# Linear attention in a twelve-stage network: two of TensorE's products and GpSimd's row gathers change places in the written order

## The chip, the cores and the metric

One core of one Trainium2 chip runs the whole program. The time is device microseconds (us) for one launch. TensorE is called PE, VectorE DVE, ScalarE ACT, GpSimd POOL and SyncE SP, as in the profile.

## The reference, cut to what matters

The network has twelve stages on x of 4096 tokens by 128 features: a feed-forward, an attention and a feed-forward, four times over. The change touches the fifth stage only, a causal linear attention with 16 heads of 8 features:

```python
x = x + 0.5 * _L1_ffn_ref(_layernorm(x), ...)      # stage 4: experts, two of 16 per token
x = x + _L1_attn_ref(_layernorm(x), ...)           # stage 5: the one that is changed
x = x + 0.5 * _L1_ffn_ref(_layernorm(x), ...)      # stage 6

def _L1_attn_ref(x, wq, bq, wk, bk, wv, bv, wo, bo):
    q = feature_map(x @ wq + bq); k = feature_map(x @ wk + bk); v = x @ wv + bv   # 16 heads of 8
    def step(carry, qkv):                          # over the tokens of one sequence
        S = S + k v^T; z = z + k                   # per head
        return (S, z), (q S) / (q z + 1e-6)
    return out @ wo + bo                           # feature_map(x) = x + 1 where x > 0, else exp(x)
```

## The kernel before, in words

x stays in on-chip memory for the whole program. It is cut into 8 chunks (NC) of 512 tokens, each of 4 tiles (TPC) of 128 tokens and two sequences of 256. Matrix products are in float32. Each engine has its own written-out instruction order, and semaphores are all that ties the orders to each other: an engine that waits holds up whatever stands behind it in its own order.

In the linear attention every engine loops over `g`, with `c, t = divmod(g, 4)`: chunk c, step t. While chunk c is scored and weighed, chunk c+1 is projected and chunk c+2 is fetched and normalised. The functions by engine:

- POOL, `att1_gpsimd`: before the loop it gathers the expert results of chunks 0 and 1 (`fetch_results`, L1319, 8 indirect DMAs each) and clears two buffers (L1749). In the loop, for chunk c: step 0 `widen(c)` (L1741), step 2 `key_heads(c + 1)` (L1731, the keys laid out by head) and then `ln_rstd(c + 2)` (L148 and L150, the reciprocal root for the normalisation, called the root here), step 3 `fetch_results(c + 4)`. The loop begins with c = -2, so that chunk 2 is gathered in it at c = -2 and chunk 7, the last, at c = 3. `fetch_results(i)` waits until DVE has written that chunk's row numbers (`name_result_rows`, L1328) and has used the buffer's earlier rows.
- DVE, `att1_vector`: `mask` each step (L1583), step 0 `invert(c)` (L1592, L1594), then `combine_results(c + 2)` (L1345, L1355, L1364) and `name_result_rows(c + 4)` (L1328); step 1 `divide(c - 1)` (L1601) and `map_qk(c + 1)` (L1550); step 2 `ln_stats(c + 2)` and `add_out(c - 1)` (L1605, L1609); step 3 `ln_apply(c + 2)` (L191), `add_bias` (L1558), `multiply_sums` (L1565) and `states` (L1572) of c + 1.
- PE, `att1_tensor`: `score` each step (L1473, 32 pairs of weight load and product) and at the step's end `weigh` of the step before (L1490, 32 pairs, and for the odd tiles the state's product L1496). Besides: step 0 `turn(c + 1)` (L203) and `sum_heads(c)` (L1449); step 1 `project(c + 1)` (L1391, L1394) and `spread(c)` (L1458); step 2 `values(c + 1)` (L1405 and L1408, 136 pairs), `turn_k(c + 1)` (L1416) and `project_out(c - 1)` (L1505); step 3 `token_values(c + 1)` (L1423), `sum_keys(c + 1)` (L1431, L1433) and, after `weigh`, `states(c + 1)` (L1441).
- ACT, `att1_scalar`: `copy_later` each step (L1666), `ln_copy` (L214), `exps` (L1675, L1677), `copy_spread` (L1701), `place_values` (L1688) and `token_keys` (L1695). For the first two chunks `place_values` waits for POOL's first `key_heads`.

`sum_heads(c)` waits for DVE's `states(c)`, `invert(c)` waits for `sum_heads(c)`, and `score` of a chunk's first step waits for that chunk's `key_heads`. All of `turn`, `project` and what follows for chunk 0 waits for its root.

Of the kernel before, what the change touches and what calls it, by code (L numbers as in the profile page):

```python
# [16 lines left out]
NC = N // CH  # L17
# [27 lines left out]
def tiles(ap, inner=P):  # L45
    return ap.rearrange("p (t d) -> p t d", d=inner)
# [1325 lines left out]
def att1_tensor(k, s):  # L1372
# [135 lines left out]
    for g in range(-TPC, STEPS1 + TPC):  # L1508
        c, t = divmod(g, TPC)
        if 0 <= g < STEPS1:  # L1510
            score(g)
        if t == 0 and 0 <= c + 1 < NC:
            turn(c + 1)
        if t == 0 and 0 <= c < NC:
            sum_heads(c)
        if t == 1 and 0 <= c + 1 < NC:
            project(c + 1)
        if t == 1 and 0 <= c < NC:
            spread(c)
        if t == 2 and 0 <= c + 1 < NC:  # L1520
            values(c + 1)
            turn_k(c + 1)
        if t == 2 and 0 <= c - 1 < NC:
            project_out(c - 1)
        if t == 3 and 0 <= c + 1 < NC:
            token_values(c + 1)
            sum_keys(c + 1)
        if 0 <= g - 1 < STEPS1:
            weigh(g - 1)
        if t == 3 and 0 <= c + 1 < NC:  # L1530
            states(c + 1)


def att1_vector(k, s):

    V, v, cols = k.nc.vector, k.v, k.w["L1_cols"]
    for at in (0, 3):
        v.count(V.tensor_scalar(cols[:, at + 1:at + 2], cols[:, at:at + 1], -1.0, None, ALU.mult))
        m = V.tensor_scalar(cols[:, at + 2:at + 3], cols[:, at:at + 1], 1.0, None, ALU.add)
    m.then_inc(k.sem("l1_cols"), 1)  # L1540

    def map_qk(c):
        for at, name in enumerate(("q", "k")):
            out, tmp = k.sb(f"l1_{name}{c % 2}", [P, CH]), k.sb(f"l1_exps{at}", [P, CH])
            V.wait_ge(k.sem("l1_exps"), 2 * c + at + 1)
            if at == 0 and c >= 2:
                V.wait_ge(k.sem("l1_weighed"), (c - 1) * TPC)
            if at == 1 and c >= 2:
                V.wait_ge(k.sem("l1_k_heads"), c - 1)
            V.scalar_tensor_tensor(out=out[:, :], in0=k.bank[1 + at][:, :], scalar=cols[:, 3 * at + 2:3 * at + 3], in1=tmp[:, :],  # L1550
                                   op0=ALU.add, op1=ALU.max).then_inc(k.sem("l1_mapped"), 1)

    def add_bias(c):
        v_tok = k.sb("l1_v_tok", [P, BPC * P])
        V.wait_ge(k.sem("l1_sums"), 4 * c + 1)
        if c:
            V.wait_ge(k.sem("l1_sums"), 4 * c - 1)
        V.tensor_tensor(tiles(v_tok[:, :]), tiles(k.bank[2][:, 0:BPC * P]),  # L1558
                        k.w["L1_bv"][:, :].unsqueeze(1).broadcast_to([P, BPC, P]), ALU.add).then_inc(k.sem("l1_parts"), 1)

    def multiply_sums(c):
        V.wait_ge(k.sem("l1_sums"), 4 * c + 2)
        if c:
            V.wait_ge(k.sem("l1_sums"), 4 * c)
        V.tensor_tensor(k.sb("l1_prod", [P, CH])[:, :], k.bank[1][:, :], k.sb(f"l1_q{c % 2}", [P, CH])[:, :],  # L1565
                        ALU.mult).then_inc(k.sem("l1_parts"), 1)

    def states(c):
        V.wait_ge(k.sem("l1_sums"), 4 * c + 3)
        if c >= 2:  # L1570
            V.wait_ge(k.sem("l1_weighed"), (c - 1) * TPC)
        V.tensor_tensor(tiles(k.sb(f"l1_state{c % 2}", [P, BPC * P])[:, :]), tiles(k.bank[2][:, S:S + BPC * P]),  # L1572
                        k.w["own_head"][:, :].unsqueeze(1).broadcast_to([P, BPC, P]), ALU.mult).then_inc(k.sem("l1_parts"), 1)

    def mask(g):

        V.wait_ge(k.sem("l1_scored"), g + 1)
        if g >= 2:
            V.wait_ge(k.sem("l1_weighed"), g - 1)
        for r in range(4):  # L1580
            if r >= 2:
                V.wait_ge(k.sem("l1_copied"), 4 * g + r - 1)
            V.tensor_tensor(own_blocks(k.sb(f"l1_weights{g % 2}_{r}", [P, CH])), own_blocks(k.bank[4 + r]),  # L1583
                            k.w["block_upto"][:, :].unsqueeze(1).broadcast_to([P, BPT, BLK]),
                            ALU.mult).then_inc(k.sem("l1_masked"), 1)

    def invert(c):
        inverse = k.sb("l1_inverse", [P, TPC * H])
        V.wait_ge(k.sem("l1_sums"), 4 * c + 4)
        if c:  # L1590
            V.wait_ge(k.sem("l1_wide"), c)
        v.count(V.tensor_scalar(inverse[:, :], k.bank[2][:, 0:TPC * H], 1e-6, None, ALU.add))  # L1592
        V.wait_ge(v.sem, v.n)
        V.reciprocal(inverse[:, :], inverse[:, :]).then_inc(k.sem("l1_inverse"), 1)  # L1594

    def divide(c):
        V.wait_ge(k.sem("l1_weighed"), (c + 1) * TPC)
        V.wait_ge(k.sem("l1_spread_in"), c + 1)
        if c:
            V.wait_ge(k.sem("l1_out"), c)  # L1600
        V.tensor_tensor(k.sb("l1_att", [P, CH])[:, :], k.bank[3][:, :], k.sb(f"l1_spread{c % 2}", [P, CH])[:, :],  # L1601
                        ALU.mult).then_inc(k.sem("l1_att"), 1)

    def add_out(c):
        v.count(V.tensor_tensor(tiles(k.chunk(c)), tiles(k.chunk(c)),  # L1605
                                k.w["L1_bo"][:, :].unsqueeze(1).broadcast_to([P, TPC, D]), ALU.add))
        V.wait_ge(v.sem, v.n)
        V.wait_ge(k.sem("l1_out"), c + 1)
        V.tensor_tensor(k.chunk(c), k.bank[0][:, :], k.chunk(c), ALU.add).then_inc(k.sem("x_done"), 1)  # L1609

    name_result_rows(k, s, 0)
    name_result_rows(k, s, 1)
    for g in range(-2 * TPC, STEPS1 + TPC):
        c, t = divmod(g, TPC)
        if 0 <= g < STEPS1:
            mask(g)
        if t == 1 and 0 <= c - 1 < NC:
            divide(c - 1)
        if t == 0 and 0 <= c < NC:
            invert(c)  # L1620
        if t == 0 and 0 <= c + 2 < NC:
            combine_results(k, s, c + 2)
            if c + 4 < NC:
                name_result_rows(k, s, c + 4)
        if t == 1 and 0 <= c + 1 < NC:
            map_qk(c + 1)
        if t == 2 and 0 <= c + 2 < NC:
            ln_stats(k, s, c + 2, s.results0 + c + 3)
        if t == 2 and 0 <= c - 1 < NC:
            add_out(c - 1)  # L1630
        if t == 3 and 0 <= c + 2 < NC:
            ln_apply(k, s, c + 2)
        if t == 3 and 0 <= c + 1 < NC:
            add_bias(c + 1)
            multiply_sums(c + 1)
            states(c + 1)


def own_blocks(buffer):

    return blocks_at(buffer, 0, BPT, BLK)
# [79 lines left out]
def att1_gpsimd(k, s):  # L1721

    G = k.nc.gpsimd

    def key_heads(c):

        kk, k_heads = k.sb(f"l1_k{c % 2}", [P, CH]), k.sb(f"l1_k_heads{c % 2}", [P, 4 * CH])
        G.wait_ge(k.sem("l1_mapped"), 2 * c + 2)
        if c >= 2:
            G.wait_ge(k.sem("l1_scored"), (c - 1) * TPC)  # L1730
        G.tensor_tensor(k_heads[:, :].rearrange("p (b j n) -> p b j n", j=4, n=BLK),  # L1731
                        tiles(kk[:, :], BLK).unsqueeze(2).broadcast_to([P, CH // BLK, 4, BLK]),
                        k.w["every_fourth"][:, :].unsqueeze(1).unsqueeze(3).broadcast_to([P, CH // BLK, 4, BLK]),
                        ALU.mult).then_inc(k.sem("l1_k_heads"), 1)

    def widen(c):

        G.wait_ge(k.sem("l1_inverse"), c + 1)
        if c:
            G.wait_ge(k.sem("l1_spread"), c)  # L1740
        G.tensor_copy(k.sb("l1_wide", [P, CH])[:, :].rearrange("p (n d) -> p n d", d=HD),  # L1741
                      k.sb("l1_inverse", [P, TPC * H])[:, :].unsqueeze(2).broadcast_to([P, TPC * H, HD])
                      ).then_inc(k.sem("l1_wide"), 1)

    fetch_results(k, s, 0)
    fetch_results(k, s, 1)
    G.wait_ge(k.sem("x_done"), s.x0)
    for n in range(2):
        G.memset(k.sb(f"l1_v_heads{n}", [P, 4 * CH])[:, :], 0.0)  # L1749
    for g in range(-2 * TPC, STEPS1 + TPC):  # L1750
        c, t = divmod(g, TPC)
        if t == 0 and 0 <= c < NC:
            widen(c)
        if t == 2 and 0 <= c + 1 < NC:
            key_heads(c + 1)
        if t == 2 and 0 <= c + 2 < NC:
            ln_rstd(k, s, c + 2)
        if t == 3 and 2 <= c + 4 < NC:
            fetch_results(k, s, c + 4)

# [1782 lines left out]
```

## Time and profile before

| | us |
|---|---|
| median of 3 runs | 3316.7 |
| lowest, highest | 3314.06, 3324.93 |
| the profiled execution | 3320.21 |
| its span, first to last instruction | 3318.9 |
| PE busy | 2633.5 |
| DVE busy | 2105.9 |
| ACT busy | 1785.2 |
| POOL busy | 1148.0 |

The linear attention runs from about 808 us of the span (its first DVE instruction) to about 1058 us. In a timeline row the columns are the start, the length, the engine, the line, the operation and its operands, how many instructions are merged, and in square brackets how long the engine had been idle and what ended that. "issue" there means that the engine waited for nothing that the profile shows; "remote" that the wait ended on a semaphore whose sender had long finished by the profile.

### The profile page before, as it was taken

How to read it: one execution, taken by the hardware profiler on the slowest of the kernel's cores; microseconds unless marked ns; L12 is line 12 of the kernel's file. 1: busy time of each engine (PE TensorE's matmuls, PEld its weight loads, DVE VectorE, ACT ScalarE, POOL GpSimd, SP SyncE). 2: the span in 40 equal slices, each digit the busy share in tenths (PEclk: the TensorE clock that was granted, in tenths of full speed). 3: DMA queues.
4: the chain of work that ended last, by engine and by line, in shares of the span. 5: the costliest groups of instructions: out<-in, count | busy, mean ns of one | idle time of the engine just before them, and what ended most of it. 6: DMA issues, size and time to landing. Idle time of an engine off the chain costs nothing. (4 is left out here: it accounts for less than half of the span.)

```text
span 3318.9 us, 67633 instructions
## 1 busy us (share of the span) xinstructions
PE 2633.5 (79%) x25429; PEld 2055.5 (62%) x25429; DVE 2105.9 (63%) x7745; ACT 1785.2 (54%) x3476; POOL 1148.0 (35%) x1567
## 2 busy tenths in 40 slices
PE   7799978677788685449489999999999867873786
PEld 4466664455566563336378888888888855542555
DVE  6577748743457734454477777777777766447666
ACT  5354436333334332226268898888898744441353
POOL 3200005621632603765562222222222226557102
PEclk9799979778768787669799999999999976885897
DMA  9300000034000143125200000000000001441000
GB/s 276 108 3 3 3 2 1 32 88 131 25 18 5 42 122 104 46 62 164 69 26 13 1 12 13 1 13 13 1 13 1 1 2 40 131 126 40 2 3 27
DMA packets 134053, 147.94 MB, mean 45 GB/s; under 512 B 14817, under 2 KB 109922, under 8 KB 133730
## 3 DMA queue, kind: packets, MB, share of 16 engines
q1 hardware_dynamic: 106306, 71.13, 7.3%
q0 software_dynamic: 27424, 72.48, 7.2%
q8 instruction: 206, 3.38, 0.4%
q14 instruction: 117, 0.96, 0.1%
HBM read 77.63 MB, written 65.93 MB: 43 GB/s over the span
## 5 line engine op out<-in xcount | busy, mean ns | idle before, releaser
L3110 POOL TENSOR_SCALAR shared_floats<-shared_floats 128x2 f32<-128x2 f32 x256 | 57.6, 225 | 718.1 <-DVE shared_floats L3101 717.6
L3032 PE MATMUL banks<-layer,shared_floats 128*128 128x128 f32 x2048 | 276.3, 279 | 0.0
L3343 ACT ACTIVATE shared_floats<-banks,layer 128x256 f32<-128x256 f32 x512 | 210.4, 471 | 93.4 <-PE banks L3019 93.2
L3032 PEld LDWEIGHTS banks<-layer,shared_floats 128*128 128x128 f32 x2048 | 254.6, 195 | 0.0
L3019 PE MATMUL banks<-shared_floats,layer 128*128 128x256 f32 x1024 | 244.0, 381 | 0.0
L3122 DVE TENSOR_SCALAR shared_floats<-banks,shared_floats 128x128 f32<-128x128 f32 x512 | 186.5, 406 | 57.8 <-POOL shared_floats L3112 57.7
L214 ACT COPY xnT<-banks 128x512 f32<-128x512 f32 x72 | 42.7, 593 | 323.7 <-PE banks L203 148.4
L1319 POOL DMA_INDIRECT results<-results,result_rows x128 | 124.1, 969 | 258.3 <-DVE result_rows L1328 110.6
L3098 DVE BATCH_NORM_STATS2 shared_floats<-banks 128x6 f32<-128x128 f32 x512 | 126.2, 289 | 129.9 <-PE banks L3032 126.3
L203 PE MATMUL banks<-ident,xn 128*128 128x128 f32 x320 | 66.1, 343 | 172.1 <-issue 94.3
L3019 PEld LDWEIGHTS banks<-shared_floats,layer 128*128 128x128 f32 x1024 | 185.9, 192 | 20.2
L3112 POOL TENSOR_TENSOR shared_floats<-shared_floats,neg_half 128x2 f32<-128x2 f32 x256 | 183.9, 718 | 21.3
L148 POOL TENSOR_SCALAR rstd<-mean_var 128x4 f32<-128x4 f32 x64 | 17.6, 275 | 461.9 <-DVE mean_var L139 460.8
L2002 DVE TENSOR_REDUCE shared_floats<-banks 128x2 f32<-128x512 f32 (+3 forms) x256 | 110.7, 485 | 95.4 <-PE banks L1866 94.1
L3308 ACT ACT_TABLE_LOAD x126 | 161.7, 1283 | 2.3
L3337 ACT ACT_TABLE_LOAD x126 | 161.7, 1283 | 2.2
L2104 ACT ACTIVATE shared_floats<-banks 128x480 f32<-128x480 f32 (+1 forms) x192 | 83.6, 488 | 143.9 <-PE banks L1873 143.9
L203 PEld LDWEIGHTS banks<-ident,xn 128*128 128x128 f32 x320 | 44.6, 174 | 187.8 <-issue 111.5
L1852 PE MATMUL banks<-shared_floats 32*128 32x128 f32 (+3 forms) x1024 | 126.2, 362 | 31.7 <-DVE shared_floats L2002 24.1
L1120 POOL DMA_INDIRECT bins<-xn,f_bin_row x128 | 125.9, 984 | 65.3 <-issue 37.5
L2758 POOL DMA_INDIRECT bins<-xn,f_bin_row x128 | 125.3, 979 | 59.0 <-issue 35.1
L1319 POOL DMA_INDIRECT results<-bins,result_rows x128 | 128.4, 1003 | 42.5 <-issue 37.2
(391 smaller groups left out, 8134.2 us busy)
## 6 DMA issues: line engine op xcount, KB each, us to landing
bins<-zero SPq DMA_DIRECT2D x1, 18176.0 KB, 86.6
shared_floats<-bins SPq DMA_DIRECT2D x32, 320.0 KB, 4.2
results<-shared_floats SPq DMA_DIRECT2D x32, 320.0 KB, 3.5
expert_weights<-in_dram_experts SPq DMA_DIRECT2D x32, 312.0 KB, 3.1
layer<-in_dram_layers SPq DMA_DIRECT2D x8, 902.0 KB, 4.8
bins<-zero SPq DMA_DIRECT2D x1, 5760.0 KB, 22.4
bins<-xn,f_bin_row POOLq DMA_INDIRECT x256
results<-results,result_rows POOLq DMA_INDIRECT x128
```

The source lines that it names most:

```text
L1120: G.indirect_dma_start(k.bins[:, :], bass.IndirectOffsetOnAxis(bin_row[:, at:at + 1], 0), xn[:, tile(at % TPC)], None).then_inc(k.sem(f"f1 ...
L1319: G.indirect_dma_start(to, None, k.results[:, :] if s.before == "ffn1" else k.bins8[:, :], bass.IndirectOffsetOnAxis(rows[:, at:at + 1], 0 ...
L1852: T.matmul(k.bank[4 + r % 2][:, at_a:at_a + wide_a], q_heads[rows32(r), blk * P:(blk + 1) * P], kk[rows32(r), half_a * BK + begin_a:half_a ...
L2758: G.indirect_dma_start(k.bins8[:, :], bass.IndirectOffsetOnAxis(bin_row[:, at:at + 1], 0), xn[:, tile(at % TPC)], None).then_inc(k.sem(f"f ...
L3019: m = T.matmul(k.bank[5 + half][:, part], w["w1"][:, tile(n)], h1[:, :], start=True, stop=True)
L3032: m = T.matmul(to, hidden[:, n * S + t * P:n * S + (t + 1) * P], w["w2"][:, tile(n)], start=False, stop=(n == NF - 1), skip_group_check=True)
L3098: v.count(V.bn_stats(stats[:, t * 6:t * 6 + 6], src[:, tile(t)]))
L3112: G.tensor_tensor(rstd[:, :], rstd[:, :], k.neg_half[:, 0:QT], ALU.pow).then_inc(k.sem(f"{name}_rstd"), 1)
L3122: m = V.tensor_scalar(xn[:, tile(t)], src[:, tile(t)], mean_var[:, t * 2:t * 2 + 1], rstd[:, t:t + 1], ALU.subtract, ALU.mult)
L3308: A.activation(exp_q[:, :], k.bank[0][:, LOW], ACT.Exp, bias=w["bq"]).then_inc(k.sem("e2_exp_q"), 1)
L3337: a.count(A.activation(spare[:, :], k.neg_one[:, :], ACT.Gelu))
L3343: m = A.activation(hidden[:, n * S:(n + 1) * S], k.bank[5 + half][:, part], ACT.Gelu, bias=w["c1"][:, n:n + 1])
```

## The change

PE computes `states(c)` in the first step of its own chunk, after the scores and ahead of `turn(c + 1)`, no longer at the end of the last step of the chunk before. `sum_heads(c)` moves behind `weigh`. DVE's `states(c)` moves with it, to the first step, ahead of `invert(c)`. DVE's `ln_apply(c + 2)` moves behind `add_bias` and `multiply_sums`. POOL's `fetch_results(c + 4)` moves from the fourth step, behind `key_heads` and the root, to the second step, ahead of both. No instruction is added or removed.

```diff
@@ att1_tensor
         if 0 <= g < STEPS1:
             score(g)
+        if t == 0 and 0 <= c < NC:
+            states(c)
         if t == 0 and 0 <= c + 1 < NC:
             turn(c + 1)
-        if t == 0 and 0 <= c < NC:
-            sum_heads(c)
...
         if 0 <= g - 1 < STEPS1:
             weigh(g - 1)
-        if t == 3 and 0 <= c + 1 < NC:
-            states(c + 1)
+        if t == 0 and 0 <= c < NC:
+            sum_heads(c)
@@ att1_vector
         if t == 0 and 0 <= c < NC:
+            states(c)
             invert(c)
...
-        if t == 3 and 0 <= c + 2 < NC:
-            ln_apply(k, s, c + 2)
         if t == 3 and 0 <= c + 1 < NC:
             add_bias(c + 1)
             multiply_sums(c + 1)
-            states(c + 1)
+        if t == 3 and 0 <= c + 2 < NC:
+            ln_apply(k, s, c + 2)
@@ att1_gpsimd
         if t == 0 and 0 <= c < NC:
             widen(c)
+        if t == 1 and 2 <= c + 4 < NC:
+            fetch_results(k, s, c + 4)
         if t == 2 and 0 <= c + 1 < NC:
             key_heads(c + 1)
         if t == 2 and 0 <= c + 2 < NC:
             ln_rstd(k, s, c + 2)
-        if t == 3 and 2 <= c + 4 < NC:
-            fetch_results(k, s, c + 4)
```

## Rows read from the trace of the kernel before

**Rows 1.** The page: PE's granted clock in 40 slices of the span, in tenths.

```profile
PEclk9799979778768787669799999999999976885897
```

**Rows 2.** Busy time by stretch: PE, PEld, DVE, ACT, POOL (instructions), PEclk, DMA.

```profile
944.70:961.70 17.00, 14.94 (x120) 11.20 (x120) 7.35 (x24) 4.43 (x11) 3.67 (x5) 0.50 0.06 16
...
961.70:969.60 7.90, 7.73 (x267) 6.22 (x269) 6.17 (x16) 6.01 (x12) 5.28 (x3) 1.00 0.02 5
969.60:981.00 11.40, 7.25 (x84) 5.63 (x77) 3.08 (x10) 1.36 (x5) 7.72 (x8) 0.75 0.17 47
1003.80:1022.80 19.00, 17.99 (x445) 14.77 (x444) 15.86 (x47) 11.63 (x27) 5.98 (x4) 1.00 0.02 4
```

**Rows 3.** Waits, 835 to 1060 us: total, times, longest.

```profile
DVE shared_floats L1583 <- remote: 22.0, 5, 6.4
```

**Rows 4.** POOL's gathers as a group, 804 to 1060 us: busy, mean ns, idle before.

```profile
L1319 POOL DMA_INDIRECT results<-results,result_rows x64 | 62.1, 970 | 128.7 <-DMA results<-shared_floats 110.1 <-issue 18.5
```

**Rows 5.** Timeline of the stage's beginning, to the second chunk's first mask.

```profile
835.45 1.05 POOL L150 TENSOR_TENSOR rstd<-rstd,neg_half 128x4 f32<-128x4 f32 x1
...
836.69 1.15 POOL L1319 DMA_INDIRECT results<-results,result_rows  x1 [0.19 <-issue]
...
837.96 1.09 PE L203 MATMUL banks<-ident,xn 128*128 128x128 f32 x4 [30.66 <-issue]
...
840.33 0.17 DVE L1328 CAST result_rows<-routes 128x8 uint32<-128x8 f32 x1
...
845.81 0.95 POOL L1319 DMA_INDIRECT results<-results,result_rows  x1 [0.30 <-issue]
...
846.77 3.62 POOL L1731 TENSOR_TENSOR shared_floats<-shared_floats,every_fourth 128x2048 f32<-128x2048 f32 x1
...
850.49 2.39 ACT L1688 ACTIVATE shared_floats<-banks 32x512 f32<-32x512 f32 x4 [4.68 <-POOL shared_floats L1731]
...
855.94 1.09 PE L1473 MATMUL banks<-shared_floats 32*128 32x128 f32 x32
...
861.90 1.04 DVE L1583 TENSOR_TENSOR shared_floats<-banks,block_upto 128x128 f32<-128x128 f32 x4 [5.28 <-remote]
...
863.36 1.93 PE L1473 MATMUL banks<-shared_floats 32*128 32x128 f32 x32 [4.94 <-issue]
...
890.06 1.04 DVE L1583 TENSOR_TENSOR shared_floats<-banks,block_upto 128x128 f32<-128x128 f32 x4 [1.27 <-PE banks L1473]
```

**Rows 6.** Timeline of chunk 3, the last that gathers, 940 to 990 us.

```profile
951.78 1.04 DVE L1583 TENSOR_TENSOR shared_floats<-banks,block_upto 128x128 f32<-128x128 f32 x4 [1.06 <-PE banks L1473]
...
958.02 0.17 DVE L1328 CAST result_rows<-routes 128x8 uint32<-128x8 f32 x1
...
964.92 0.95 PE L1408 MATMUL banks<-L_wqkvo,xnT 128*32 128x32 f32 x87
...
969.65 1.09 POOL L1319 DMA_INDIRECT results<-results,result_rows  x1 [0.19 <-issue]
...
974.57 0.21 PE L1490 MATMUL banks<-shared_floats 128*32 128x32 f32 x1 [0.52 <-issue]
...
981.01 1.54 PE L1473 MATMUL banks<-shared_floats 32*128 32x96 f32 x24 [0.35 <-issue]
...
982.58 1.04 DVE L1583 TENSOR_TENSOR shared_floats<-banks,block_upto 128x128 f32<-128x128 f32 x4 [0.92 <-PE banks L1473]
```

**Rows 7.** Timeline of chunk 5, which gathers nothing, 996 to 1045 us.

```profile
1003.17 0.71 PE L1441 MATMUL banks<-shared_floats 128*128 128x128 f32 x4
...
1004.97 1.03 DVE L1583 TENSOR_TENSOR shared_floats<-banks,block_upto 128x128 f32<-128x128 f32 x4 [0.63 <-PE banks L1473]
...
1006.33 0.23 DVE L1592 TENSOR_SCALAR shared_floats<-banks 128x64 f32<-128x64 f32 x1 [0.32 <-PE banks L1449]
...
1006.91 0.49 PE L1496 MATMUL banks<-shared_floats 128*128 128x128 f32 x2
...
1010.01 0.88 DVE L1583 TENSOR_TENSOR shared_floats<-banks,block_upto 128x128 f32<-128x128 f32 x4
```

## The prediction

> **What bounds the kernel now.** The page first: a slice is 83 us, and in the eleventh to thirteenth, which hold this stage, PE's clock is granted at 0.7, 0.6 and 0.8 of full [rows 1]. The rest of the program is not touched by the change. I then read the cycle of a chunk, from the first mask of one to the first mask of the next, in the timeline. A cycle with gathers takes 982.58 - 951.78 = 30.8 us [rows 6], one without 19.0, nearly all of it PE's work at full clock [rows 2]. Nothing that PE has to compute differs between the two.
>
> Where the 12 us go is seen in the stretches [rows 2]. From the first gather to PE at speed again (969.6 to 981.0) PE gets only some 80 pairs of load and product through in 11.4 us, while in the 7.9 us before it got 267. In this time PE waits for "issue" again and again, as for 0.52 us ahead of one single product at 974.57 [rows 6], and DVE's masks wait for "remote", up to 6.4 us [rows 3]: PE's products are over, and their signals come late. Both end about 1.5 us after the eighth gather. At the stage's beginning it is the same: the first scores run at 855.94 and last 1.09, and the mask that waits for them begins at 861.90, when the third train of gathers is over [rows 5]. I take from this as a fact of the trace, whatever its cause, that a train of gathers lets some 160 PE instructions (84 and 77) through in 11.4 us. The second cost follows: the clock falls to 0.50 about 6 us after the train has begun and stays there for 17.0 us (944.7 to 961.7, one cycle of 30.8 us before the one shown, so that its train began at 938.9), after PE had run in short pieces; then it is 1.00 [rows 2].
>
> So the bound of this stage is PE's order of work, as it is cut by the trains, and for chunk 0 the chain root, turn, project, keys by head, values.
>
> **The change part by part.** The sum is made against the profiled execution, 3320.2 us (span 3318.9), which is 3.5 above the median of 3316.7; I add the difference to the median.
>
> *Chunk 0's root behind a train.* The first gathers inside the loop (chunk 2's, c = -2) now stand ahead of the first root. Their row numbers are long written and POOL is free after its clearing, at about 835.1 (its root's second operation is at 835.45), so they start there. A train is 8 gathers; from 836.69 to 845.81 + 0.95 it takes 10.1 us [rows 5], and mean and spacing (970 ns and 0.30) are the same for all [rows 4]. The root, over at 836.50 before, is over at 846.5, and turn, which PE had idled 30.66 us for, goes from 837.96 to 848.0: **+10.0**. Nothing covers it: PE, ACT and DVE all stand behind that root.
>
> *Chunk 0's keys behind a second train.* Chunk 3's row numbers come with DVE's order at 840.33 + 10.0 = 850.4. POOL then gathers until 860.5 and only after that lays out keys by head, 3.6 us, until 864.1; before, they were ready at 850.4 [rows 5]. ACT's placing of values waits for exactly that [rows 5], so it moves by 13.7, and so do token values, sums of keys and scores: 855.94 + 13.7 = 869.6, ended at 870.7. The mask follows at once now, since no train is on; DVE has `ln_apply` ahead of it, which costs 0.8. So the first mask is at 871.5, against 861.90: **+9.6**. The second train's price is thus mostly given back by the late signal that goes away.
>
> *The first step.* PE's work is only reordered (states in, sum of heads out behind weigh), but `invert` now waits for states (0.7) and for all that lay from the first mask to the end of the state product, 1007.40 - 1004.97 = 2.4: 3.2 us at full clock, with the mask 0.1 behind the scores. Before it was 1006.33 - 1004.97 = 1.4 [rows 7]. DVE's own `states`, 0.4, fits in between. Behind `invert` on DVE stand the combining of results, the row numbers and the next mask, 1010.01 - 1006.33 = 3.7 us later [rows 7]. So the row numbers are there and the train starts 7.1 us into the cycle, not 17.9 [rows 6]. In a cycle without a train the second mask, 5.0 us after the first, is bound by just this DVE chain [rows 7]; with `invert` 1.9 later and the states product's 0.7 no longer ahead of the scores, I book **+1.2** for chunk 5, the one with such a chain, no gathers and full clock. For chunks 6 and 7, without combining, DVE is done before PE's next scores are (1.2 us of slack after 3.2 us): 0.
>
> *The gathers' new place, chunks 1 to 3.* Count from the first mask. Train at +7.1, PE at speed at +18.5. The 80 pairs let through are spread (4), weigh (32), scores (32) and the first dozen of the 136 of values. Before, the train fell on the tail of scores, token values, sums of keys, weigh and states, whose columns are many and whose instructions few; now it falls on the steps richest in instructions. The rest of values takes 1.6 us: +20.1. From there to the next first mask PE has turn, project out, weigh, scores, token values, sums of keys, weigh, scores: about 7.5 us at full clock. If the clock falls 6 us after the train's start and stays low for 17.0, until +30.1, then 10 us of that run at half clock, where these products take 1.77 times as long (scores 1.93 for 1.09 [rows 5]): 5.7 us of work, and 1.8 us are left after it. The cycle ends near +31.9, against 30.8: **+1.1 each, +3.3**. From both sides: if all of the 11.4 us were covered by ACT's and DVE's chains the cycle could fall to that without gathers plus its longer first step, 20 us (-10.8 each); if the train held values for its whole length and the tail ran all at half clock it would be 34 (+3.2). I stay near the rows that I counted from, since the stretch of 11.4 us and the low 17.0 us repeat in every cycle with gathers.
>
> *Chunk 0's cycle.* It was 890.06 - 861.90 = 28.2 us (its first mask came late, behind a train) [rows 5]; it is now 31.9 less the 0.8 that its first mask is late: **+2.9**. *Chunk 4* gathers nothing but began before in what the last train left, its end and the low clock: 1004.97 - 982.58 = 22.4 [rows 6, 7]. Now the train is over long before: 19.0 + 1.2 = 20.2: **-2.2**.
>
> *Keys by head and the root later in the cycle.* They follow the train, at +17.2 to +22.5; the keys are needed at about +30 and the root by `ln_apply` at about +30: 7 us of cover, gone only if the cycle falls below 24. Moving `ln_apply` behind the sums is then needed, and costs nothing. PE's wait for `add_bias` ahead of states goes, inside the stretch of the train, worth nothing while that bounds.
>
> Sum: 9.6 + 1.2 + 3.3 + 2.9 - 2.2 = **+14.8 us**; profiled 3335.0, and by the median 3331.5: I say **3331**.
>
> One rule speaks against my reading. The Trainium skill (Runtime: NRT & Kernel Launch, Instruction fetch mechanics) says that an engine refills its instructions by a queue of its own while it runs, mostly hidden; by it a train would cost PE nothing wherever it stands, and only the first two parts would remain. The trace does not agree: 80 pairs in 11.4 us against 267 in 7.9 [rows 2].
>
> **The rivals.** *The trains find cover (faster).* One mechanism: in the second step PE's wait for masks, exps and mapped queries is there anyway, so the train's stall lies in it, and the next scores no longer run in the train's end. For it: the third and first steps' products all ran in the train's end or at half clock before, and chunk 4's cycle shows that a cycle not ended by a train is 22.4. Against it: nothing waits 11 us in the second step. Price: the cycle falls to 24 in chunks 1 to 3 (-6.8 each) and to 23.2 in chunk 0 (-5.0): -25.4, and with +9.6, +1.2 and -2.2 a change of -16.8: 3300. It decides from a cycle of 28.2, where 4 cycles pay back those 8.6 us, and is seen in the time below 25.7. Chance 0.14.
>
> *Position costs nothing, the beginning does.* The cycle stays at 30.8 (30.0 in chunk 0, +1.8) and the rest is as above: 9.6 + 1.8 + 1.2 - 2.2 = +10.4, 3327. For it: the stretch of 11.4 us is as long in either place. Chance 0.25.
>
> *Values starve.* PE at 5 or 6 instructions per us instead of the mean 14, as in the single product at 974.57 amid half-microsecond waits [rows 6]: the train then lets only part of scores through, `mask` of the third step and all of ACT's placing come behind it, and a cycle is 34.5: 3 x 3.7 + 5.5 = 16.6, with the same 8.6 +25.2: 3342. Chance 0.17.
>
> *The gathers do not move.* If the row numbers were written only in the third step they would start where they did. They are written at 958.02, 11.6 us before the gathers' start [rows 6]; and the first one has its numbers before the root. It would give 3317, as before. Chance 0.03.
>
> A rule of the Trainium skill (SBUF — State Buffer, "SBUF: two separate sides", its warning on DMA that VectorE blocks) adds to the starving case: VectorE in some modes keeps GpSimd from writing descriptors, and the second step has more of such work than the fourth. The trace shows the first gather of a train at 1.15 us beside `ln_apply`, 0.2 over the others [rows 5]; by the rule a train would grow by that or so, 1 us over all trains.
>
> **How the numbers follow.** Forecast 0.41, cover 0.14, position costs nothing 0.25, starving 0.17, no move 0.03. A change below 0.3%, about 10 us, can't be told from none. Slower: forecast 0.36 of its 0.41, starving 0.17, the position case about half, 0.12: 0.65. Faster: cover 0.10 of its 0.14. Same: the rest, 0.25. The likeliest case's own range is 3325 to 3338; the range that holds 8 in 10 is 3314 to 3345, without most of the cover case and the worst of starving.
>
> **What would show it.** Right: the first root ends at about 846.5 and turn begins at 848; the first mask near 871; in the cycles trains begin about 7 us after the first mask; PE's issue waits lie in scores and values and not in states and the next scores; the low clock covers the third and fourth steps; keys and root after each train, with nobody waiting for them; chunk 4's cycle about 20. Wrong: if the first turn is not 10 us late, if a cycle with gathers is under 28 us, or if the clock stays full through a train.

## The result, and the profile after

The changed kernel takes 3329.18 us (median of 20 runs, 3319.37 to 3343.92), the kernel before 3321.49 (20 runs, 3311.96 to 3334.42), run beside it. The ratio is 1.0024 with a 95% interval of 1.0013 to 1.0036: about 8 us slower, between 4 and 12. The forecast of 3331 is 2 us off, but the change was forecast at +14.8 and measured at +7.7. That the stage answers for it is seen on its own length, from its first gather to the first product of the stage behind it (L203, at 1061.69 before and 1066.09 after): 250.1 us before and 260.6 after, +10.5 in the two profiled executions (spans 3318.9 and 3323.1; the rest of the program differs by 6 the other way, nearly all of it ahead of the stage). These two kernels on this chip are called the first pair below.

The table is worked out from the timelines. "turn" and "mask" are the first `turn` and first mask after the stage's first gather, then the cycles of chunks 0 to 6 (first mask to first mask), the last chunk (its first mask to that product), and the stage's length.

```
                 turn  mask  cycles of chunks 0 to 6                    last  stage
before           26.4  50.3  28.2  30.8  31.0  30.8  22.4  19.0  17.8   19.9  250.1
after            36.1  61.8  28.0  29.1  29.9  28.7  22.5  20.0  17.6   23.3  260.6
```

The page after, PE's granted clock (before: [rows 1]); the stage lies in slices eleven to thirteen:

```profile
PEclk9799989788678787679799999999999977885897
```

Stretches of after, columns as in [rows 2]: the stretch at half clock before the first mask, one train of gathers, the half clock around it, the full clock behind it, and the half clock in the last chunk.

```profile
853.30:867.00 13.70, 8.51 (x140) 7.42 (x139) 2.01 (x6) 2.94 (x5) 6.07 (x5) 0.50 0.04 11
961.60:973.00 11.40, 8.28 (x87) 4.91 (x87) 2.24 (x4) 3.19 (x6) 9.20 (x9) 0.54 0.19 48
962.50:976.20 13.70, 11.42 (x207) 7.96 (x208) 4.26 (x15) 4.97 (x11) 11.19 (x11) 0.50 0.16 41
976.20:993.20 17.00, 15.09 (x307) 12.60 (x309) 11.11 (x34) 8.79 (x21) 1.61 (x2) 1.00 0.01 2
1047.90:1054.70 6.80, 6.56 (x105) 6.15 (x106) 2.45 (x7) 1.62 (x5) 0.00 (x0) 0.50 0.01 2
```

The second line is the counterpart of the 11.4 us in [rows 2]: 87 loads and 87 products where it was 77 and 84. The train lets as little through in its new place, at 0.54 of the clock, as in its old one at 0.75.

Waits of DVE and the gathers as a group in the stage (before: [rows 3, 4]), from the view of waits and that of groups:

```profile
DVE shared_floats L1583 <- remote: 19.7, 3, 7.9
```

```profile
L1319 POOL DMA_INDIRECT results<-results,result_rows x64 | 61.7, 964 | 144.4 <-DMA results<-shared_floats 110.2 <-issue 17.8 <-DVE result_rows L1328 16.4
```

The gathers cost the same. New is that POOL waits 16.4 us for the row numbers: the gathers start 0.7 us after these are written. The timeline of the stage's beginning (before: [rows 5]):

```profile
839.30 1.05 POOL L150 TENSOR_TENSOR rstd<-rstd,neg_half 128x4 f32<-128x4 f32 x1
...
841.60 1.08 PE L203 MATMUL banks<-ident,xn 128*128 128x128 f32 x4 [40.41 <-issue]
...
844.94 1.09 POOL L1319 DMA_INDIRECT results<-results,result_rows  x1 [4.60 <-DVE result_rows L1328]
...
854.84 3.61 POOL L1731 TENSOR_TENSOR shared_floats<-shared_floats,every_fourth 128x2048 f32<-128x2048 f32 x1
858.54 2.39 ACT L1688 ACTIVATE shared_floats<-banks 32x512 f32<-32x512 f32 x4 [9.09 <-POOL shared_floats L1731]
...
865.30 1.86 PE L1473 MATMUL banks<-shared_floats 32*128 32x128 f32 x32
...
867.24 1.04 DVE L1583 TENSOR_TENSOR shared_floats<-banks,block_upto 128x128 f32<-128x128 f32 x4
```

The root ends at 840.35, and only then does turn run; keys by head start when the second train ends, ACT places values when they are done, and the first scores run at half clock (1.86 us, where [rows 5] has 1.09), with the mask behind them at once.

The timeline of one cycle of after, the one of chunk 3, the last that gathers (before: [rows 6]):

```profile
954.16 1.04 DVE L1583 TENSOR_TENSOR shared_floats<-banks,block_upto 128x128 f32<-128x128 f32 x4
...
957.12 0.23 DVE L1592 TENSOR_SCALAR shared_floats<-banks 128x64 f32<-128x64 f32 x1 [1.59 <-PE banks L1449]
...
960.87 0.88 DVE L1583 TENSOR_TENSOR shared_floats<-banks,block_upto 128x128 f32<-128x128 f32 x4
...
961.64 1.09 POOL L1319 DMA_INDIRECT results<-results,result_rows  x1 [2.94 <-DVE result_rows L1328]
...
962.44 1.27 PE L1490 MATMUL banks<-shared_floats 128*32 128x128 f32 x32 [1.99 <-issue]
...
972.97 1.83 PE L1408 MATMUL banks<-L_wqkvo,xnT 128*32 128x32 f32 x116 [1.09 <-issue]
...
973.08 1.04 DVE L1583 TENSOR_TENSOR shared_floats<-banks,block_upto 128x128 f32<-128x128 f32 x4 [7.92 <-remote]
...
976.89 0.76 PE L1490 MATMUL banks<-shared_floats 128*32 128x128 f32 x32
...
982.83 1.04 DVE L1583 TENSOR_TENSOR shared_floats<-banks,block_upto 128x128 f32<-128x128 f32 x4
```

The train begins 7.5 us after the first mask. When it is over, at 971.5, 120 of the 128 products of values are still to run, 116 of them from 972.97 on; the mask of the third step waits 7.92 us for a signal that is late (the scores that it needs ended at 966.5). From weigh at 976.89 on PE is at full clock, and the next first mask comes 28.7 us after the last.

### The profile page after: what moved, and what is told of

It reads as the page before. It is cut to its first block and busy times, and to the rows that moved or that the text cites. A ratio compares the mean times of both kernels' runs of the same rounds, so it can differ in the third digit from the quotient of the medians.

```text
span 3323.1 us, 67633 instructions
## 1 busy us (share of the span) xinstructions
PE 2620.4 (79%) x25429; PEld 2047.7 (62%) x25429; DVE 2100.8 (63%) x7745; ACT 1785.5 (54%) x3476; POOL 1147.4 (35%) x1567
## 5 line engine op out<-in xcount | busy, mean ns | idle before, releaser
L203 PE MATMUL banks<-ident,xn 128*128 128x128 f32 x320 | 64.4, 336 | 182.4 <-issue 104.0
L3019 PEld LDWEIGHTS banks<-shared_floats,layer 128*128 128x128 f32 x1024 | 185.5, 191 | 20.1
L203 PEld LDWEIGHTS banks<-ident,xn 128*128 128x128 f32 x320 | 44.0, 171 | 197.7 <-issue 121.5
## 6 DMA issues: line engine op xcount, KB each, us to landing
layer<-in_dram_layers SPq DMA_DIRECT2D x8, 902.0 KB, 4.7
```

The costliest lines, as they stand in the source:

```text
L3019: m = T.matmul(k.bank[5 + half][:, part], w["w1"][:, tile(n)], h1[:, :], start=True, stop=True)
```

## The experiments

The experiments ran on three chips on which the kernel before takes 3224 to 3230 us, some 95 less than in the first pair; the stage has 47.5 of them (202.6 us instead of 250.1), the rest lies in stages that the change does not touch. I call these "the other chips"; that it is the chip, and not something else of the time of those runs, is inferred. Ratios are to the kernel before on the same chip (differences in us are worked out from them). e1 to e4 ran on one of these chips, b0, a0, e5 and e6 on the second, g1 to g4 on the third. The table goes on, with numbers of the same kind.

```
                 turn  mask  cycles of chunks 0 to 6                    last  stage
b0 before        26.4  46.9  20.6  19.5  20.1  19.5  19.3  19.0  17.7   19.9  202.6
a0 after         36.2  61.8  23.9  25.0  24.0  23.2  22.3  20.0  17.6   23.3  240.9
e1 gathers       36.1  61.8  25.0  25.2  26.9  26.9  22.8  18.9  17.7   19.9  245.1
e2 products      26.3  45.6  20.2  24.6  20.2  24.3  19.6  20.0  17.6   23.4  215.3
e3 late first    26.4  45.8  23.0  23.1  24.0  24.9  22.3  20.0  17.6   23.0  223.7
e4 early first   36.1  61.9  19.3  19.9  19.6  19.7  18.9  20.9  17.7   19.9  217.8
e5 before, 1/8   26.4  48.5  19.3  18.9  20.0  18.7  18.6  19.3  17.7   20.3  201.2
e6 after, 1/8    36.1  61.8  22.2  24.1  20.3  24.1  19.6  22.5  17.6   20.3  232.5
g1 sum_heads     36.1  61.5  22.9  23.9  23.5  24.0  19.0  19.5  18.3   21.9  234.5
g2 + apply       36.1  62.1  22.0  23.7  22.8  23.2  21.6  19.6  18.1   19.9  233.1
g3 two a step    26.4  45.6  21.0  21.2  19.4  19.2  20.0  19.1  17.7   19.9  203.2
g4 beginning     20.0  46.7  25.5  20.6  20.4  20.7  18.6  18.9  17.7   19.9  209.0
```

**The two halves.** Before with the gathers alone moved (e1), and after with the gathers where they were (e2).

```diff
# e1, against before (e2 is the reverse, against after)
+        if t == 1 and 2 <= c + 4 < NC:
+            fetch_results(k, s, c + 4)
...
-        if t == 3 and 2 <= c + 4 < NC:
-            fetch_results(k, s, c + 4)
```

> The kernel before with the gathers alone moved to the second step. Theory A (the beginning costs, the cycles give back): the first turn 10 us late and the first mask 11 to 12 us late, cycles with a train 1 to 2 us shorter than 30.8, the whole +5 to +8 us. Theory B (the gathers' place is worth nothing in the cycles, and what they gained in the changed kernel came from the products' new order): the first mask as late, cycles 30.8, the whole +11 us or more.

> The changed kernel with the gathers back in the fourth step behind the root; only PE's and DVE's orders are changed. Theory A: the first mask as before, cycles within 0.5 us of 30.8, the sum of heads costs about 1 us in chunk 5: the whole 0 to +3 us. Theory B: cycles 29 to 30, the whole -5 us.

Measured: e1 3269.05, 1.0122 [1.0103, 1.0140], +39 us; e2 3244.60, 1.0045 [1.0029, 1.0061], +15. Theory A had +5 to +8 and 0 to +3, theory B +11 or more and -5, all for cycles of 30.8, which this chip does not have. Both halves are dearer here than the whole change was in the first pair, and the gathers need a part of the other half: the move of `ln_apply` behind the sums. In e1 it waits for the root, which is now behind train and keys, and `add_bias` and PE's states wait behind it, with all that follows at half clock:

```profile
936.52 1.04 POOL L150 TENSOR_TENSOR rstd<-rstd,neg_half 128x4 f32<-128x4 f32 x1
937.60 1.12 DVE L191 TENSOR_SCALAR xn<-x,mean_var,rstd 128x128 f32<-128x128 f32 x4 [2.40 <-POOL rstd L150]
938.63 0.42 DVE L1558 TENSOR_TENSOR shared_floats<-banks,L_bv 128x256 f32<-128x256 f32 x1
...
939.10 1.22 PE L1441 MATMUL banks<-shared_floats 128*128 128x128 f32 x4 [2.26 <-DVE shared_floats L1558]
```

In e2 the second mask is late, 7.3 us after the first where b0 has 5.6, and in the two cycles of 24.6 and 24.3 the clock is low for some 10 us each (873.3 to 883.5 and 917.7 to 927.9). The timeline of e2, second step of chunk 1: weigh runs after a wait of 1.74 at half clock, 1.29 us for 0.76.

```profile
871.84 0.88 DVE L1583 TENSOR_TENSOR shared_floats<-banks,block_upto 128x128 f32<-128x128 f32 x4
...
873.41 1.29 PE L1490 MATMUL banks<-shared_floats 128*32 128x128 f32 x32 [1.74 <-issue]
```

The wait alone does not bring the low clock: in chunk 2 the same weigh comes after 1.99 us of idling (897.46), runs in 0.76, and the clock stays at 1.00.

**The beginning and the cycles apart.** The trains of chunks 2 and 3 stand ahead of the first root and the first keys; those of chunks 4 to 7 stand in the cycles. e3 is after with the first two where they were, e4 is before with only these two moved.

```diff
# e3, against after
-        if t == 1 and 2 <= c + 4 < NC:
+        if t == 1 and 4 <= c + 4 < NC:
             fetch_results(k, s, c + 4)
...
+        if t == 3 and 2 <= c + 4 < 4:
+            fetch_results(k, s, c + 4)
# e4, against before
+        if t == 1 and 2 <= c + 4 < 4:
+            fetch_results(k, s, c + 4)
...
-        if t == 3 and 2 <= c + 4 < NC:
+        if t == 3 and 4 <= c + 4 < NC:
             fetch_results(k, s, c + 4)
```

> The changed kernel, but chunks 2 and 3 are gathered in the old place, behind root and keys by head; chunks 4 to 7 in the second step. Theory A: the first mask as before, cycles as in the changed kernel (28.6 to 29.9): the whole -3 to -6 us against before, 11 less than the changed kernel. Theory B: the same if only the order of the products gained; both fall if the 11 us at the beginning come back.

> The kernel before with only chunk 2's and 3's gathers moved to the second step. Both theories: first turn +10 us, first mask +11 us, cycles 30.8: the whole +10 to +11 us. If it is under +6 the beginning is not what the changed kernel lost.

Measured: e3 3249.75, 1.0063 [1.0044, 1.0082], +20; e4 3243.63, 1.0047 [1.0030, 1.0064], +15. The table shows a clean cut: e4 has the first mask of after (61.9) and the cycles of before (b0), e3 has the first mask of before (45.8) and about the cycles of after on such a chip (a0). The beginning is a price of its own, 15 us here (10 to 11 expected); e3 was expected at -3 to -6, with the cycles of the first pair, and shows instead that here the cycles are dearer too.

**Both kernels on another chip, and without the trains.** b0 is before and a0 is after, unchanged. e5 and e6 are the two with one gather instead of eight for each of chunks 4 to 7.

```diff
# e5, against before (e6 the same, against after)
+KEPT = 1
...
-            fetch_results(k, s, c + 4)
+            fetch_results(k, s, c + 4, (0, K1 if c + 4 < 4 else KEPT))
```

> The kernel before once more, for its profile on the chip of this group of runs. If this chip is of the kind of the first experiments (the kernel before at 3230 us and not 3321), I expect cycles of 19 to 20 us with a train, as in the experiment with only the first trains early, and PE hardly short of instructions in them; if of the kind of the first result, 30.8.

> The changed kernel once more, beside the kernel before on this chip. Theory A (trains cost where PE's order is rich in instructions, and how much depends on the chip): on a chip like the first result's +8 us; on a chip like the first experiments' the gathers' move costs 6 us in each of four cycles beside the 11 at the beginning, +35 to +50 us. Theory B (the cost is the same on every chip): +8 us.

> The kernel before, which fetches only one of the 8 groups of rows for each of chunks 4 to 7 (their combined results are left incomplete). Cost of the trains in the old place: on a chip like the first result's, theory A says that cycles 0 to 3 fall from 28.2 to 30.8 to about 20, -40 us in all, and the clock stays full. On one like the first experiments', nearly nothing, 0 to -5 us. Theory C (the long cycles are the combining of results and not the trains): no change on either.

> The changed kernel, with only one of the 8 groups of rows fetched for each of chunks 4 to 7. What is left against the one before with the same cut is the beginning (+11 us) and the later sum of heads (+1 per cycle with combining, 6 of them): +15 to +17 us against that kernel. The trains' price in the new place is the changed kernel's time less this: 4 x 9 us on a chip like the first result's, 4 x 6 on one like the first experiments'.

Measured: b0 3221.40 (one run, beside 13 with a median of 3224.14); a0 3258.99, 1.0106 [1.0089, 1.0123], +34, which is e3 and e4 together (20 + 15); e5 3218.47, 0.9983 [0.9968, 0.9998], -6; e6 3251.25, 1.0079 [1.0060, 1.0097], +25. That is 31 to 33 above e5, where 15 to 17 were expected, and only 8 or 9 below a0, where 24 were (the beginning's 15 stay in e6, which fetches chunks 2 and 3 whole).

So on the other chips trains do not starve PE. Stretches of b0: its seven cycles, of which the first four gather, and the length of one train.

```profile
857.00:994.00 137.00, 125.85 (x3068) 103.62 (x3068) 104.17 (x302) 77.43 (x184) 66.17 (x55) 1.00 0.07 19
897.00:908.00 11.00, 10.79 (x195) 8.79 (x194) 8.54 (x28) 3.83 (x11) 8.81 (x9) 1.00 0.19 50
```

195 pairs in 11.0 us at a clock of 1.00, where the first pair of profiles has 80 to 87 in 11.4 ([rows 2], and above). Taking seven gathers of eight away (e5) gains at most 10 us of the whole kernel there. The Trainium skill (Runtime: NRT & Kernel Launch, Instruction fetch mechanics) says that an engine's instructions are refilled by a queue of its own, mostly hidden. The trace of b0 agrees, with its 195 pairs; those of the first pair do not, with their 80 to 87. Each reading holds on its own chip, and no run shows that the fetching of instructions is what fails in the first pair.

With nothing to hide in, the change costs more in the cycles, and two causes are there for it. The first is POOL's order. The timeline of a0, one cycle of 25.0 us from first mask to first mask:

```profile
886.34 0.87 DVE L1583 TENSOR_TENSOR shared_floats<-banks,block_upto 128x128 f32<-128x128 f32 x4
...
895.45 1.09 POOL L1319 DMA_INDIRECT results<-results,result_rows  x1 [2.94 <-DVE result_rows L1328]
...
904.35 0.94 POOL L1319 DMA_INDIRECT results<-results,result_rows  x1 [0.30 <-issue]
...
905.32 3.61 POOL L1731 TENSOR_TENSOR shared_floats<-shared_floats,every_fourth 128x2048 f32<-128x2048 f32 x1
...
909.03 1.09 PE L1473 MATMUL banks<-shared_floats 32*128 32x128 f32 x32 [1.06 <-issue]
...
910.30 1.11 DVE L191 TENSOR_SCALAR xn<-x,mean_var,rstd 128x128 f32<-128x128 f32 x4 [2.29 <-POOL rstd L150]
...
911.33 0.88 DVE L1583 TENSOR_TENSOR shared_floats<-banks,block_upto 128x128 f32<-128x128 f32 x4
```

The keys by head end at 908.93 and the scores that read them begin at 909.03. The cycle began at 886.34, the train at 895.45: 9.1 to the row numbers and POOL's start on them, 9.9 of gathers, 3.6 of keys, 2.4 to the mask are 25.0, all of the cycle. Of the 9.1, the half clock from 886.8 to 897.0 has 1.8: the next cycle, 23.9, has 7.3 there. The last 2.4 are not only the scores, which end at 910.1: DVE waits for the root behind the keys and runs `ln_apply` ahead of the mask, some 1.2 us more. In all four gathering cycles of a0 the first mask comes 2.4 us after the keys by head end, where b0 has 5.9 to 7.4; in the cycle after the one shown (keys end 932.88, scores 932.98) PE waited only 0.32 for them.

The second cause is the order of the products, and e6 shows it alone: without the trains the first mask comes 5.6 to 9.5 us after the keys, so POOL bounds nothing, and the cycles are still 22.2, 24.1, 20.3 and 24.1, where e5 has 18.7 to 20.0. PE idles 1.98 us ahead of the second step's weigh in each of the last three; in the two of 24.1 the clock is at half from there on for some 10 us (891.7 to 902.0 and 936.1 to 946.3), in the one of 20.3 it stays at 1.00. So either cause makes long cycles without the other, and taking one away gives back only part of the price.

**Three attempts to mend it, and one on the beginning.** g1 is after with `sum_heads` back behind `turn`. g2 is e1 with DVE's `ln_apply` behind the sums.

```diff
# g1, against after
         if t == 0 and 0 <= c + 1 < NC:
             turn(c + 1)
+        if t == 0 and 0 <= c < NC:
+            sum_heads(c)
...
-        if t == 0 and 0 <= c < NC:
-            sum_heads(c)
# g2, against e1
-        if t == 3 and 0 <= c + 2 < NC:
-            ln_apply(k, s, c + 2)
...
+        if t == 3 and 0 <= c + 2 < NC:
+            ln_apply(k, s, c + 2)
```

> The changed kernel with sum of heads again right behind turn, ahead of weigh. Theory A (weigh ahead of it makes invert, the combining and the second mask late, PE idles over 2 us in the second step and the clock falls): where trains do not starve PE, the cycles of 23 to 25 fall to about 20 to 21 and the stage's end loses its 3.4 us; the whole 15 us or more under the changed kernel, +15 to +20 against before. Theory B (the train beside the second step makes them long): cycles stay at 23 to 25, the whole +33. Where trains starve PE: +8 less the end's 3.4 and 1 per cycle.

> The kernel before with the gathers in the second step, as in the first experiment, and DVE's ln_apply behind add_bias and multiply_sums. Theory A (there the late root held ln_apply, add_bias behind it and with it PE's states for 2 us, and the clock fell): cycles of 25 to 27 fall to 20 to 21, and with the beginning's 15 us the whole is +15 to +20 us instead of +39. Theory B (the train's place): it stays at +35 to +39. Where trains starve PE: cycles 28 to 29, +8.

Measured: g1 3260.26, 1.0107 [1.0087, 1.0128], +35: nothing gained against a0's +34, as theory B had it (theory A had +15 to +20), though the cycle without gathers falls from 22.3 to 19.0. g2 3254.16, 1.0086 [1.0065, 1.0106], +28: `ln_apply` out of the way gives back 11 or 12 of e1's 39, between the two theories. What is left in both is POOL's order, here in g2 and then in g1:

```profile
919.09 3.61 POOL L1731 TENSOR_TENSOR shared_floats<-shared_floats,every_fourth 128x2048 f32<-128x2048 f32 x1
...
922.81 1.54 PE L1473 MATMUL banks<-shared_floats 32*128 32x128 f32 x32 [2.05 <-issue]
```

```profile
921.39 3.61 POOL L1731 TENSOR_TENSOR shared_floats<-shared_floats,every_fourth 128x2048 f32<-128x2048 f32 x1
...
925.10 1.93 PE L1473 MATMUL banks<-shared_floats 32*128 32x128 f32 x32 [2.58 <-issue]
```

Twice more the scores begin 0.1 us after the keys by head end (922.70 and 925.00), after a wait of over 2 us, whatever the order of PE and DVE. In all four gathering cycles of both the first mask comes 2.4 or 2.5 us after the keys' end, as in a0.

g3 is before with the gathers of chunks 4 to 7 two a step, each pair after that step's scores; g4 is before with the two buffers cleared ahead of chunk 1's train, the first root after two gathers of that train, and chunk 2's train in two halves around the second root.

```diff
# g3, against before
+        first = c + 4 if t == 3 else c + 3
+        if 4 <= first < NC:
+            if t == 2:
+                later = True
+            else:
+                later = False
+                G.wait_ge(k.sem("l1_scored"), g + 1)
+                fetch_results(k, s, first, (2 * ((t + 1) % 4), 2 * ((t + 1) % 4) + 2))
...
-        if t == 3 and 2 <= c + 4 < NC:
+        if later:
+            G.wait_ge(k.sem("l1_scored"), g + 1)
+            fetch_results(k, s, first, (6, 8))
+        if t == 3 and 2 <= c + 4 < 4:
             fetch_results(k, s, c + 4)
# g4, against before
-    fetch_results(k, s, 1)
...
+    fetch_results(k, s, 1, (0, 2))
+    ln_rstd(k, s, 0)
+    fetch_results(k, s, 1, (2, K1))
...
+        if t == 2 and c == -1:
+            fetch_results(k, s, 2, (0, 4))
...
+        if t == 2 and c == -1:
+            fetch_results(k, s, 2, (4, K1))
```

> The kernel before with the eight gathers of each of chunks 4 to 7 spread over four steps, two after each step's scores. If a train starves PE by its length, cycles of 30.8 fall to 21 to 24 on a chip like the first result's: -25 to -35 us. On one where trains cost nothing: 0, within 3 us.

> The kernel before with POOL's order changed at the beginning alone: the buffers cleared after the first train, the root of chunk 0 after two gathers of the second, and chunk 2's gathers behind the first keys by head, in two halves around chunk 1's root. If the beginning is bound by what stands ahead of the first root and the first keys, the first turn comes 7 us earlier and the first mask 4 to 6 us: -4 to -6 us on either kind of chip. If DVE's combining of chunk 1, which waits for the second train, bounds it, 0 to -1.

Measured: g3 3227.26, 0.9998 [0.9984, 1.0012], no change; where trains do not starve PE there is nothing for it to save, so it says nothing on the chip of the first pair. g4 3235.34, 1.0021 [1.0008, 1.0034], +7, against an expected gain. Its first turn is 6.4 us earlier, its first mask is not:

```profile
829.38 0.98 POOL L1319 DMA_INDIRECT results<-results,result_rows  x1
...
834.49 1.05 POOL L150 TENSOR_TENSOR rstd<-rstd,neg_half 128x4 f32<-128x4 f32 x1
...
835.57 1.32 DVE L191 TENSOR_SCALAR xn<-x,mean_var,rstd 128x128 f32<-128x128 f32 x4 [8.84 <-POOL rstd L150]
836.60 0.42 DVE L1558 TENSOR_TENSOR shared_floats<-banks,L_bv 128x256 f32<-128x256 f32 x1
...
837.07 1.22 PE L1441 MATMUL banks<-shared_floats 128*128 128x128 f32 x4 [0.93 <-DVE shared_floats L1558]
838.22 1.93 PE L1473 MATMUL banks<-shared_floats 32*128 32x128 f32 x32
```

The four gathers that I had put ahead of the second root hold `ln_apply` of chunk 1 up, and `add_bias`, states and the first scores, at half clock, stand behind it. The mechanism is the one of e1. The other half of the train then lies in chunk 0's cycle, 25.5 instead of 20.6. No kernel was faster than before by more than its interval, leaving aside e5, which fetches less.

## Why the prediction was right, and where not

The time was right in part by luck. The change was forecast at +14.8 and measured at +7.7; the forecast stood on a median of 3316.7 from three runs, and the 20 runs of the pair have 3321.49, 4.8 higher. Within the sum, too, terms were off in opposite ways. Times after the stage's first gather are compared, since the stage itself starts 6 us earlier in the profile of after.

- *Root behind a train, +10.0.* Turn is at 36.1 instead of 26.4: +9.7. Right, and e4 shows it alone.
- *First mask, +9.6.* It is +11.5. The keys by head end 14.2 later (predicted 13.7) and the late signal was given back as said. What I left out is the clock: it fell to 0.50 at 853.3, after PE had run in pieces, and the products from token values to the first scores ran in it. On the other chips there is no late signal to give back: +15 there.
- *The train at +7.1, PE at speed at +18.5, values done at +20.1.* It began at +7.5 and values were done at +20.5 (974.7). 87 pairs got through, predicted about 80. Right, with one thing of the starving rival: the third step's mask came behind the train (7.92 us of waiting), though its scores had run.
- *The rest of the cycle, 11.8 us, of which 10 at half clock: wrong.* This is the step that failed: "if the clock falls 6 us after the train's start and stays low for 17.0, until +30.1". The clock fell at 962.5, just when the train began, after PE's idle 2 us ahead of weigh (the second mask was late, since combining now lies behind the later `invert`), and rose at 976.2. In the four cycles with gathers it fell 0.9 to 3.5 us after the train's start, not 6, and stayed low for 13.7 us, not 17.0. So it lay over the train, where PE gets little done anyway, and hardly over the tail. The tail thus took 8.1 us (974.7 to 982.8). The cycles of chunks 1 to 3 changed by -1.7, -1.1 and -2.1, -4.9 together, where I had +3.3, and that of chunk 0 by -0.2, where I had +2.9. That puts the cycle, 29.2 on average, below the 30.8 of "position costs nothing", on the way to "the trains find cover" but far from it. That rival's sum, +10.4, meets the stage's +10.5 by number only: its first four cycles are 6.9 us too dear, and first mask, chunk 4 and the last chunk 7.6 too cheap. By the prediction's own sign of being wrong, a cycle under 28 us, chunk 0's 28.0 (27.99) is at the edge.
- *Chunk 4, -2.2.* It is +0.1: the clock was low in 993.2 to 1000.1, which I had not counted. *Chunk 5, +1.2.* It is +1.0, by the chain that I named: `invert` 3.0 us after the mask, the second mask at +6.6.
- *The last chunk, 0.* It is +3.4 (23.3 for 19.9). With `invert` later, the spreading of results waits 0.56 us for POOL's `widen`, PE waits 0.59 ahead of weigh, and 6.8 us run at half clock (the last of the stretches above). e2, e3 and a0 have it (23.0 to 23.4), e1, e4 and b0 not (19.9), so the order of products is needed for it. It is not enough: e6 has that order and the same two waits, its clock stays at 1.00, and its last chunk takes 20.3. What pulls the clock down there is open. It was missing from my sum, as 0 for chunks 6 and 7.
- *Keys and root later, 7 us of cover, gone only below a cycle of 24.* It held on the first chip, where scores come 6.5 us after the keys end. On the other chips, with cycles of 20 to work on, the cover is gone and this order bounds the cycles of 22.0 to 25.0 of a0, g1 and g2. `ln_apply` behind the sums does not "cost nothing" there, since it stands ahead of the mask.

The sum of after is 11.5 - 0.2 - 4.9 + 0.1 + 1.0 - 0.2 + 3.4 = 10.7, the stage's +10.5 but for rounding; mine was 14.8. I had the first four cycles 11.3 us too dear, and first mask, chunk 4 and the last chunk together 7.6 too cheap.

Not settled is why a train starves PE on one chip and hardly on others, nor when the clock falls. The records name the starving only as "issue" and "remote". No experiment ran on the chip of the first pair, and whether e3, g3 or e5 would be faster there was not tried.

## What to carry to other kernels

When a long block of one engine's queue is moved ahead of short operations that others wait for, count the cycle that is left if the block's own side effects vanish: what must be done ahead of the block, the block, the short operation and its first user in a row are a floor, and here it was 23 to 25 us against cycles of 20. When two parts of a change can each lengthen the same cycle, test each without the other: taking the trains out of the changed kernel gave back only 8 or 9 of 34 us, 15 of which lay at the beginning. Shift the users as well (the apply behind the sums gave back 11 or 12 us), and look at the prologue apart, where nothing covers the block. A cost that one profile shows as stalls without a named releaser may belong to that chip; a change whose worth hangs on it needs a second chip.

## What the runs showed of the hardware

- A train of eight indirect gathers takes GpSimd 9.9 to 10.1 us (964 ns each, 0.30 between). TensorE gets 77 to 87 pairs of load and product through in 11.4 us around it in the first pair, with a mask's signal up to 7.9 us late, and 195 in 11.0 us on another chip, at a granted clock of 1.00. The same program takes 3321 us on the first and 3224 to 3230 on the others.
- In after TensorE's clock was at 0.50 right behind an idle of 1.99 us (962.44), for 13.7 us, and in e2 behind one of 1.74 us (873.41), for 10.2. Such an idle is not enough: after 1.91 us at 1013.49 in after, 1.99 at 897.46 in e2 and 1.98 at 915.62 in e6 the clock stayed at 1.00. Two waits of 0.56 and 0.59 us ahead of weigh in the last chunk had 6.8 us at half clock behind them in after and none in e6. At half clock the 32 products of scores take 1.93 us for 1.09. In b0 the clock keeps 1.00 from 857 to 994, and in a0 it falls in the cycles of chunks 1 to 4 and in the last chunk.
